# A scatter ring of three places with two token tiles each, and output rows normalized in pairs

## The reference

```python
x = x + attention0(layernorm(x)) + ffn0(layernorm(x))      # 1st layer, dense
xn = layernorm(x)
# 2nd layer, attention
xl = ln(xn, ln1_w, ln1_b)
qk, v = silu(xl @ Wqk.T + bqk), silu(xl @ Wv.T + bv)
quad_q, lin_q, quad_k, lin_k = rope(qk * gamma + beta)
attn = relu(quad_q @ quad_k.T / 64 + bias) ** 2            # in groups of 64
lin_out = lin_q @ (lin_k.T @ v / n)
out = silu(xl @ Wg.T + bg) * (attn @ v + lin_out)
att = ln(out @ Wo.T + bo, ln2_w, ln2_b)                    # the rows that YS and YF make
# 2nd layer, experts
weights, indices = top_k(softmax(xn @ Wg2.T), 2)
y_e = (silu(h1) * h3) @ W2e.T + b2e                        # h1, h3 of expert e
return x + att + sum(weights * y_e)
```

## Time and profile before

| | |
|---|---|
| median of 3 runs | 1101.35 us (1100.79 to 1102.86) |
| profiled execution | 1101.88 us, its span 1100.2 us |
| PE busy | 1053.0 us, 96% of the span |
| VectorE busy | 781.5 us, 71% |
| POOL busy | 432.7 us, 39% |
| mean granted clock of TensorE | 0.987 of full speed |

### The profile page before, as it was taken

How to read it: one execution, slowest core, us unless ns; L and a number is a source line. 1 busy time by engine, 2 the same in 40 slices (tenths; PEclk the granted TensorE clock), 3 DMA queues, 4 the chain that set the end, 5 groups by cost and what they waited for, 6 DMA issues and landing times.

```text
span 1100.2 us, 20434 instructions
## 1 busy us (share of the span) xinstructions
PE 1053.0 (96%) x6338; PEld 913.0 (83%) x6338; DVE 781.5 (71%) x1741; ACT 393.8 (36%) x770; POOL 432.7 (39%) x416
## 2 busy tenths in 40 slices
PE   5999999999999998999987999999999999999995
PEld 3899989999999998867765788888888888878774
DVE  5688787888787768766734777777777777754755
ACT  2636363555445454432210232322322322432310
POOL 2845553554446423037665000101001000188886
PEclk9999999999999999899998999999999999999998
DMA  9264573556366446416675456424355251355556
GB/s 273 99 211 132 177 243 119 173 139 237 109 216 189 148 160 194 122 64 193 210 211 157 162 192 207 157 99 146 114 182 188 72 180 54 111 98 88 69 96 143
DMA packets 113588, 168.61 MB, mean 153 GB/s; under 512 B 17104, under 2 KB 87376, under 8 KB 113360
## 3 DMA queue, kind: packets, MB, share of 16 engines
q1 hardware_dynamic: 93136, 120.09, 35.2%
q0 software_dynamic: 20352, 47.23, 15.7%
HBM read 96.14 MB, written 71.14 MB: 152 GB/s over the span
## 4 chain that ended last, share of the span: by engine, by line
PE 81%; DVE 5%; DMA 5%; issue 5%; POOL 3%; DVEq 0%; POOLq 0%; SPq 0%
PE wide L549 20%; PE wide L1912 17%; PE bank L549 12%; PE bank L1912 9%; PE wide L1410 4%; PE bank L1937 3%; POOL slot_rows_scratch L1359 3%; DMA slot_rows_scratch<-ring,slot 2%; DMA ring<-xn_scratch 2%; PE bank L1410 2%; PE bank L640 1%; PE bank L1905 1%; PE wide L1470 1%; PE wide L1483 1%; PE wide L1494 1%
## 5 line engine op out<-in xcount | busy, mean ns | idle before, releaser
L1912 PE MATMUL wide<-expert_ring,xsT 128*128 x642 | 170.5, 401 | 2.9 <-DVE xsT L2001 2.1
L1912 PEld LDWEIGHTS wide<-expert_ring,xsT 128*128 128x128 f32 x642 | 113.3, 188 | 23.2 <-issue 3.7
L1970 ACT ACTIVATE gsT<-bank 128x512 fp32r<-128x512 f32 x71 | 42.6, 601 | 242.1 <-PE bank L1937 242.1
L1795 POOL DMA_DIRECT2D expert_ring<-experts_scratch x24 | 17.3, 720 | 262.6 <-issue 134.9
L2013 DVE TENSOR_TENSOR slots_h<-wide,expert_bias 128x512 f32<-128x512 f32 x71 | 49.1, 692 | 67.7 <-PE wide L1912 67.5
L1359 POOL DMA_INDIRECT slot_rows_scratch<-ring,slot x64 | 67.2, 1049 | 66.7 <-DVE slot L1746 31.7
L532 POOL TENSOR_TENSOR folded_matrix<-fold,folded_matrix 128x512 fp32r<-128x512 f32 x48 | 64.0, 1341 | 42.9 <-ACT folded_matrix L726 40.1
L549 PE MATMUL wide<-xnT,w 128*128 128x512 f32 x234 | 60.3, 399 | 0.0
L1912 PEld LDWEIGHTS bank<-expert_ring,gsT 128*128 128x128 f32 x432 | 56.1, 189 | 3.5 <-issue 0.3
L529 POOL TENSOR_TENSOR rsa<-vea,half 128x1 f32<-128x1 f32 x32 | 21.3, 666 | 94.9 <-DVE vea L908 93.8
L549 PE MATMUL wide<-xnT,pT 128*128 128x512 f32 (+2 forms) x288 | 58.5, 348 | 0.0
(11 more groups left out here) (284 smaller groups left out, 2584.1 us busy)
## 6 DMA issues: line engine op xcount, KB each, us to landing
experts_scratch<-folded_matrix SPq DMA_DIRECT2D x24, 1024.0 KB, 5.1
expert_ring<-experts_scratch POOLq DMA_DIRECT2D x24, 1024.0 KB, 6.0
raw<-in_expert_weights SPq DMA_DIRECT2D x24, 512.0 KB, 7.3
xs_ring<-slot_rows_scratch SPq DMA_DIRECT2D x71, 128.5 KB, 2.3
slot_results_scratch<-ys_ring SPq DMA_DIRECT2D x71, 128.0 KB, 2.1
slot_rows_scratch<-zeros SPq DMA_DIRECT2D x23, 385.5 KB, 7.2
ring<-xn_scratch SPq DMA_DIRECT2D x16, 514.0 KB
xn_scratch<-u SPq DMA_DIRECT2D x16, 512.0 KB, 6.9
```

The costliest lines, as they stand in the source:

```text
L1912: ins = mm(o, parts[i], moving, start=(first and q == 0), stop=(last and q == 2))
L1970: return nc.scalar.activation(o, i, ACT.Copy)
```

## The change

The ring gets three places of two tiles (`RINGS = 3`, now counted in pairs). The third lies in the first half of `u`, whose rows are free once PE has turned them (`UT:3`), so `RG:2` waits for that. `RG:m` now waits for pair m-3. The power is taken for two tiles at once: `vey` gets four places, POOL has `YS` at odd numbers only, and VectorE has `YF` at odd numbers only, each of which finishes two tiles. `YS` of an even tile on VectorE ends with its statistics (1687 before); its aggregation is issued in the odd tile's `YS`, and both variances are then written by one instruction. The lists of VectorE and POOL are changed accordingly.

```diff
-RINGS = 4
+RINGS = 3
...
-    keep["ring"] = Room(nc, at + 16 * 1024, 9 * 1024).take("ring", [P, RINGS, TOPK * ROW])
+    keep["ring"] = [Room(nc, at + 16 * 1024 + 4128 * i, 4128).take(f"ring{i}", [P, 2, TOPK * ROW]) for i in range(2)]
+    keep["ring"].append(Room(nc, *old["rows"]).take("ring2", [P, 2, TOPK * ROW]))
...
-                i, pair = 2 * n % RINGS, slice(2 * n * P, (2 * n + 2) * P)
-                if 2 * n >= RINGS:
-                    for at in (i, i + 1):
-                        sp.wait_ge(moved[at], 32 * (2 * n // RINGS))
+                i, pair = n % RINGS, slice(2 * n * P, (2 * n + 2) * P)
+                if n >= RINGS:
+                    sp.wait_ge(moved[i], 2 * 16 * TOPK * (n // RINGS))
+                elif n == RINGS - 1:
+                    sp.wait_ge(t_done, T_AT[("UT", TPB // 2 - 1)] + 1)
...
             if kind == "YS":
-                pool.wait_ge(var_ready, T0 + n + 1)
-                nc.gpsimd.tensor_tensor(rsy[:, n % 4:n % 4 + 1], vey[:, n % 2:n % 2 + 1], keep["half"][:, 0:1], ALU.pow
-                                        ).then_inc(rstd_ready, 1)
+                pair = slice(n % 4 - 1, n % 4 + 1)
+                pool.wait_ge(var_ready, (T0 + n + 1) // 2)
+                nc.gpsimd.tensor_tensor(rsy[:, pair], vey[:, pair], keep["half"][:], ALU.pow).then_inc(rstd_ready, 1)
...
             elif kind == "YS":
-                i = n % 2
-                if n >= 4:
-                    hold(dve, v_held, x_ready, T0 + n - 3)
-                tt(y[:, n % 4, :], g_full(dve, ("YY", n))[:, 0:DIM], row("bo"), ALU.add).then_inc(g_free(("YY", n))[0], 1)
+                i, odd = n % 4, n % 2
+                if n >= 4 and not odd:
+                    hold(dve, v_held, x_ready, T0 + n - 2)
+                tt(y[:, i, :], g_full(dve, ("YY", n))[:, 0:DIM], row("bo"), ALU.add).then_inc(g_free(("YY", n))[0], 1)
+                if odd:
+                    hold(dve, v_held, v_step, measured[n - 1])
+                    own(nc.vector.bn_aggr(mvy[:, i - 1, :], sty[:, 0, :]), wait=False)
                 hold(dve, v_held, *g_free(("YY", n)))
-                own(nc.vector.bn_stats(sty[:, i, :], y[:, n % 4, :]))
-                own(nc.vector.bn_aggr(mvy[:, n % 4, :], sty[:, i, :]))
-                if n >= 2:
-                    dve.wait_ge(rstd_ready, T0 + n - 1)
-                ts(vey[:, i:i + 1], mvy[:, n % 4, 1:2], EPS, None, ALU.add).then_inc(var_ready, 1)
+                measured[n] = own(nc.vector.bn_stats(sty[:, odd, :], y[:, i, :]), wait=False)
+                if odd:
+                    hold(dve, v_held, v_step, measured[n])
+                    own(nc.vector.bn_aggr(mvy[:, i, :], sty[:, 1, :]))
+                    ts(vey[:, i - 1:i + 1], mvy[:, i - 1:i + 1, 1], EPS, None, ALU.add).then_inc(var_ready, 1)
             elif kind == "YF":
-                i = n % 4
-                dve.wait_ge(rstd_ready, T0 + n + 1)
-                own(stt(out=y[:, i, :], in0=y[:, i, :], scalar=mvy[:, i, 0:1], in1=row("ln2_w"), op0=ALU.subtract,
-                        op1=ALU.mult))
+                dve.wait_ge(rstd_ready, (T0 + n + 1) // 2)
+                for i in (n % 4 - 1, n % 4):
+                    own(stt(out=y[:, i, :], in0=y[:, i, :], scalar=mvy[:, i, 0:1], in1=row("ln2_w"), op0=ALU.subtract,
+                            op1=ALU.mult), wait=False)
                 hold(dve, v_held, x_biased, B0 + n // TPB + 1)
-                if half:
-                    hold(dve, v_held, *all_added("x", n))
-                stt(out=x[n // TPB][:, n % TPB, :], in0=y[:, i, :], scalar=rsy[:, i:i + 1], in1=x[n // TPB][:, n % TPB, :],
-                    op0=ALU.mult, op1=ALU.add).then_inc(x_ready, 1)
+                for t, step in ((n - 1, steps[0] - 1), (n, steps[0])):
+                    i, rows = t % 4, x[t // TPB][:, t % TPB, :]
+                    hold(dve, v_held, v_step, step)
+                    if half:
+                        hold(dve, v_held, *all_added("x", t))
+                    stt(out=rows, in0=y[:, i, :], scalar=rsy[:, i:i + 1], in1=rows, op0=ALU.mult, op1=ALU.add
+                        ).then_inc(x_ready, 1)
```

More of the change, by code:

```diff
@@ L221, in tile_rooms @@
     keep["sty"], keep["mvy"] = a.take("sty", [P, 2, 6]), a.take("mvy", [P, 4, 2])
-    keep["vey"], keep["rsy"], keep["half"] = a.take("vey", [P, 2]), a.take("rsy", [P, 4]), a.take("half1", [P, 1])
+    keep["vey"], keep["rsy"], keep["half"] = a.take("vey", [P, 4]), a.take("rsy", [P, 4]), a.take("half1", [P, 2])
     a = Room(nc, *old["pT"])
@@ L299, in layer0 @@
     xb = keep["u"]
+    old["rows"] = (keep["u_at"], 8 * 1024)
     old["pT"] = (place(), 16 * 1024)
@@ L1085 @@
     "scalar": "GA:15:18",
-    "vector": "YS:13:1 YS:14:2 YF:11:1 YS:15:4 YF:12:19 YF:13:1 YF:15:2",
-    "gpsimd": "YS:10:1 YS:13:1",
+    "vector": "YS:13:1 YS:14:3 YS:15:4 YF:13:20 YF:15:2",
+    "gpsimd": "YS:9:1 YS:13:1",
     "sync": "RG:15:12",
@@ L1215, in attention @@
         w_high, w_split, offset_step = sem("l1_weights_high"), sem("l1_weights_split"), sem("head_offsets_step")
-        ring_in = [sem(f"ring_in{i}") for i in range(RINGS // 2)]
+        ring_in = [sem(f"ring_in{i}") for i in range(RINGS)]
         moved = keep["moved"]
@@ L1309, in unit @@
                     sp.wait_ge(*dense["gates_stored"])
[L1310 to L1315 removed]
+                i, pair = n % RINGS, slice(2 * n * P, (2 * n + 2) * P)
[3 more added lines that the diff above has]
+                    sp.wait_ge(t_done, T_AT[("UT", TPB // 2 - 1)] + 1)
+                sp.dma_start(ring[i][:], scr["xn1"][pair].rearrange("(t p) k d -> p t (k d)", p=P)
+                             ).then_inc(ring_in[i], 16)
             elif kind == "LZ":
@@ L1586, in vector, with own @@
         tt, ts, stt = nc.vector.tensor_tensor, nc.vector.tensor_scalar, nc.vector.scalar_tensor_tensor
-        def own(ins):
+        measured = {}
+        def own(ins, wait=True):
             steps[0] += 1
             ins.then_inc(v_step, 1)
-            hold(dve, v_held, v_step, steps[0])
+            if wait:
+                hold(dve, v_held, v_step, steps[0])
+            return steps[0]
         def unit(un):
@@ L1782, in attention, with moved_in_all @@
             "heads_done": (headB_ready, H0 + 2 * NB), "output_done": g_finished(("YY", NB * TPB - 1))}
+def moved_in_all(i):
+    return 2 * 16 * TOPK * len(range(i, TILES // 2, RINGS))
 def expert_of_rank(pool, keep, j):
@@ L1879, in unit @@
                 for i in range(RINGS):
[L1880 removed]
+                    hold(pool, loader_held, keep["moved"][i], moved_in_all(i))
                 loaded(e, range(3))
```

43 lines of the change are left out of this document (21 added, 22 removed).

## The result

Measured beside the kernel before on one chip: **1088.03 us** median (4 runs, 1085.05 to 1088.31) against 1102.11 (4 runs, 1100.79 to 1103.55). The ratio is 0.9861, 95% interval 0.9848 to 0.9874: faster by 14 us. 1084 was predicted, within 1080 to 1092. The profiled execution took 1088.31 us, with a span of 1086.6 against 1100.2 before, 13.6 less. One finding stands over all that follows: the same program gave 1086.81 on a second chip and 1112.06 on a third, where it is *slower* than before. The experiments come to that.

The account below looks back on a forecast made before the run. PE was taken to bound the kernel, except at a few waits. Slot tile 0 13.6 us earlier, with -1.2 + 2.1 + 0.7 + 0.8 + 1.5, made 17.5 off 1101.88: 1084.4, less 0.5, so 1084; range 1080 to 1092.

Parts of the forecast that it names:

- The ring hides the round trip: Scatter on POOL: three places cover 11.55 us against 9.2 to 11.3; all 17.6 us of waits go, end at 574.9.
- rival 1: Scatter and reloads: transfers get slower as they are packed; at a 14 us round trip the time is 1091; chance 0.15.
- PE's gaps before the hand-over vanish: Before slot tile 0: four gaps, 6.70 us, and 1.7 of clock go; PE ready at 582.9 instead of 591.27.
- The cover of 4.0 us: At slot tile 0: PE is ready 4.0 us after the rows can be there, covering everything put at nothing on POOL.
- The hand-over: At slot tile 1: PE waits 0.7 to 1.5 us for VectorE's list, taken as 1.2, too short to lower the clock.
- The clock's 2.1 us come back: After the hand-over, 596 to 601 us: the clock was 0.58, and the 2.1 us this cost are regained.
- rival 2: Before the hand-over: `YF` pairs wait for powers behind scatters; one returning stall costs 5.4 us, giving 1089 to 1090; chance 0.10.
- Stage 3: After PE's last product: the last stores start some 1.5 us earlier, bounds 0 to 2.6.
- The sum: Whole kernel: slot tile 0 turned 13.6 us earlier, with -1.2 + 2.1 + 0.7 + 0.8 + 1.5, total 17.5 us.
- The rule against it: Ring: by 2.0 us plus bytes at 436 GB/s, two places nearly hide the round trip; a third brings nothing.
- Rival 3: Stage 3: `YF` pairs wait for powers behind gathers, handing PE tiles late; a 20 us loss gives 1104; chance 0.03.

Follow-up runs that it names:

- ring_only_again: Kernel before with the three-place ring alone (single output rows, no pairs), run again on another chip: 1091.08 us, ratio 0.9883 to the kernel before.
- change_third: The changed kernel word for word, run a third time, on another chip beside the kernel before: 1112.06 us, ratio 1.008.
- tile0_before_ys13: Changed kernel with slot tile 0's low part on VectorE one unit earlier, before `YS:13`: 1111.15 us, ratio 1.0074 to before; 1083.95 us on another chip.

## Why the prediction was right, and where it was off

- *The ring hides the round trip*: right in effect, not in its own numbers. Of 17.6 us 15.6 were saved, and the scatter ends at 576.98 instead of 574.9. The transfers did slow down, as rival 1 said. The round trip that begins at 559.26 takes 6.27 + 5.86 us and, with the hand-overs, 12.9 us until POOL goes on at 572.18, over the 11.55 us that three places cover, in the stretch where the DMA share is 0.89. It costs 1.4 us: the idle time of 1.73 less the 0.30 that pass before every scatter. The one from 540.30, with 5.95 + 6.36 us, costs nothing: its load has landed at 552.63, and POOL, with two powers and a unit `LE` in between, first needs the place at 555.14. So only the later one cost anything, and rival 1 came true in part, at an end 2.1 us later, and PE did not notice: its data were there.
- *PE's gaps before the hand-over vanish*: right. 6.70 us and the clock's 1.7, predicted readiness at 582.9, measured 582.45.
- *The cover of 4.0 us*: enough for PE's data, not for VectorE. With the 3.98 us from POOL's end to the turn, the rows could be turned at 580.96, 1.5 us before PE came: 2.5 of the 4.0 us were used up. VectorE's `YF:9` waited 0.62 us for the power behind the last scatter (577.00 with 2.31 us).
- *The hand-over*: the step that failed. I took 1.2 us of waiting at slot tile 1, "too short ... to bring the clock down". The wait is 2.58 in both traces, and the clock fell behind it in one of two. The rows had shown 1.55 and 2.92 us, and nothing between them. VectorE's list itself was right: from `XB:1` at 576.45 to 587.00 it is 10.55 us with the wait of 0.62, so 9.93 of work against 9.9. PE's five products take 575.54 to 584.56, 9.02 us, the short end of my 9.0 to 9.8, where the forecast's own terms give 1.5 and not 1.2. On top come the 0.62 for the power on POOL, 0.30 because `OO:15` begins that much behind `YY:11` (575.84), and 0.15 to hand the tile over: 2.57.
- *The clock's 2.1 us come back*: of the two traces, only in the one where it does not fall again.
- *Pairs make VectorE wait for POOL* (rival 2): it waits 13.4 us in 5 pieces, up to 6.60 at 548.60, where I had "2 to 3 us". PE lost 0.23 us by it before the hand-over: its queue had work. The prediction priced one stall of 9.14 us at 5.4; this one of 6.60 cost next to nothing.
- *Stage 3*: the last product starts 13.86 us before the span's end; before it was 14.94 (1085.26 of 1100.2), and in `ring_only_again` (1074.41 of 1089.1) it is 14.69. The change gains 1.1 us there, 0.8 of them by the pairs, against 1.5.
- *The sum*: 17.5 predicted against 13.6 measured in spans. At slot tile 0 it is 14.06 (13.6 predicted); to the turn of `slots_g` -2.3 instead of -1.2 + 2.1 + 0.7 = +1.6; behind that +1.8 instead of +2.3. So the miss of 3.9 us is the hand-over; the other two differences cancel. Where the clock holds, the profiled execution takes 1084.38, the 1084 of the forecast, and that is in part luck: its first scatter starts 1.1 us earlier than in the trace of before (480.27 against 481.40), in work that the change leaves as it was. From the first scatter to the last stores it gains 16.4 us (597.8 against 614.2), not 17.5, mostly since the wait at slot tile 1 is 1.4 us longer than the forecast's.
- *The rule against it*: the Trainium skill (DMA: Bandwidth & Descriptors, section "Anatomy of one DMA — SWDGE (gpsimd) path") gives 2.0 us plus bytes at 436 GB/s, as an estimate 2.3 and 3.2 us here. The section is on transfers issued by GpSimd, so it bears on the scatter, and on SP's load only by analogy. The trace disagrees, with 4.60 and 3.74 us at the mildest. By the rule a two-place ring would have hidden the round trip and a third place brought nothing; in `ring_only_again` it brought 13 us.
- *What no rival had*: that the same program can be slower than before on another chip. Rival 3 had the direction, with 1104, but the wrong mechanism and place. The forecast's 0.03 for slower was too sure: of the three comparisons of this very program one came out slower.

## What to carry to other kernels

A third place in a ring pays when the time from a place's last scatter to its next full load is longer than the work of the other places; take that round trip from the busiest stretch, and expect it to grow when the pauses go (11.3 us at most before, 12.9 after). Where two engines hand over, count what each has left from the same instant: behind a wait of 2.58 us 2.4 us of clock were lost in one trace and not in the other, and one step moved on VectorE brought the wait to 1.04 us or less. Line two traces up at the last point that the change can't have moved, here the first scatter, before their ends are compared: 1.6 us between two traces of one program lay ahead of it. And a gain that packs the queues should be measured on more than one chip before it is kept: one comparison, at 0.9861 with a narrow interval, said nothing of the 1.008 on another.

## What the runs showed of the hardware

- With scatters issued back to back every 1.28 us and reloads beside them, VectorE went on 7.7 us after the work that it waited for had ended (`change_third`; 11.4 in `tile0_before_ys13`), and ScalarE 16.8 us later than in another run of the same program. On two of the four numbered chips all 23 executions with a three-place ring took 1108 to 1118 us; the 34 elsewhere, the result's four among them, 1083 to 1094. With two places the delay was 2.4 to 2.6 us and hidden in the traces that have it. Records of signals were missing from the traces in the same stretch (480 against 1353 from 480 to 560 us, and from the first landings on), while the transfers moved as much as without the stall (197 and 200 GB/s from 491 to 510 us). The cause stays open, as does whether it is the chip or the occasion: each chip was used once.
- The granted clock fell to 0.57 (587 to 595 us, half speed for most of it) behind a 2.58 us gap of PE in one execution and stayed at 1.00 behind the same gap in another; it stayed there in the four profiles in which VectorE's work was moved (PE's gaps of 0.3 to 1.04 us at the hand-over, and 1.45 or 1.46 a turn later), and it fell in that of `ring_only_again` (0.64 from 587 to 596 us, behind 2.21 us at slot tile 0). In `change_third` a gap of 1.88 us at slot tile 1 did not bring it down.
- One 132 KB scatter took 5.95 to 6.27 us to land and one 526 KB load 5.86 to 6.36 us at a DMA share of 0.83 to 0.89, against 4.60 and 3.74 at the start of the scatter.
